# Delta rule: queries convolved after the projection instead of inside it, on ScalarE and VectorE

## The reference, cut to what matters

```python
y = conv_general_dilated(x, w[:, None, :], window_strides=(1,), padding=[(KS - 1, 0)], feature_group_count=C)
return silu(y)                                   # per channel: w[0]*x[t-3] + w[1]*x[t-2] + w[2]*x[t-1] + w[3]*x[t]
...
q = conv_silu(x @ Wq, conv_q).reshape(bsz, seq_len, H, KD)      # H = 8 heads, KD = 128
k = conv_silu(x @ Wk, conv_k).reshape(bsz, seq_len, H, KD)
v = conv_silu(x @ Wv, conv_v).reshape(bsz, seq_len, H, VD)      # VD = 32
q = l2norm(q)
k = l2norm(k)
def step(state, inp):                            # scanned over the tokens
    retained = einsum('bhvk,bhk->bhv', state, k_t)
    state = a4 * (state - b4 * rk) + b4 * vk     # rk, vk: outer products of retained and of v_t with k_t
    o_t = einsum('bhvk,bhk->bhv', state, q_t)
```

## Time and profile before

| | us |
|---|---|
| median of 3 runs | 4452.96 (4449.75 to 4459.58) |
| the profiled execution: its own time | 4450.96 |
| its span, first to last instruction | 4449.0 |
| TensorE busy in the span | 3796.8 (85%) |
| VectorE | 2365.0 (53%) |
| ScalarE | 1509.0 (34%) |
| GpSimd | 736.4 (17%) |
| taps (L2008): 1024 records, first and last start | 2768.5 and 4225.0 |
| mean granted TensorE clock over the span | 0.808 |

### The profile page before, as it was taken

One profiled execution on the slowest core, in us unless ns is written; L12 is line 12 of the kernel. 1 busy time (PEld: TensorE's weight loads), 2 busy tenths in 40 slices (PEclk: granted clock), 3 DMA queues, 4 the chain that ended last, 5 costly groups with the idle time before them and its releaser, 6 DMA issues. The chain is left out here.

```text
span 4449.0 us, 124857 instructions
## 1 busy us (share of the span) xinstructions
PE 3796.8 (85%) x55640; PEld 2398.6 (54%) x55640; DVE 2365.0 (53%) x6027; ACT 1509.0 (34%) x2783; POOL 736.4 (17%) x724
## 2 busy tenths in 40 slices
PE   4877775999948887878787795999999999999986
PEld 2336662444325555556565442566666666666672
DVE  3757773332268777777777111244444444444445
ACT  2643332555432222222222142333333333333323
POOL 1212221000011112121211000222222222222210
PEclk9886666999955556555655697999999999999967
DMA  2000001322000000000000001000000000000000
GB/s 80 0 1 1 1 1 30 47 38 38 17 1 3 3 3 3 3 3 3 3 3 3 16 1 58 1 2 2 2 2 2 2 2 2 2 2 2 2 2 21
DMA packets 18968, 45.93 MB, mean 10 GB/s; under 512 B 4864, under 2 KB 8321, under 8 KB 17409
## 3 DMA queue, kind: packets, MB, share of 16 engines
q1 hardware_dynamic: 18432, 37.95, 3.6%
HBM read 35.71 MB, written 2.23 MB: 9 GB/s over the span
## 5 line engine op out<-in xcount | busy, mean ns | idle before, releaser
L2008 PE MATMUL ps<-d_hp,d_w_qk 128*128 128x512 f32 x1024 | 546.3, 629 | 2.7 <-DVE d_hp L2265 2.7
L1227 PE MATMUL ps<-g_Q,g_K 32*32 32x32 f32 (+1 forms) x12288 | 272.7, 249 | 21.9 <-issue 7.5
L1227 PEld LDWEIGHTS ps<-g_Q,g_K 32*32 32x32 f32 x12288 | 238.3, 136 | 65.0 <-PE ps L1227 39.0
L2086 POOL TENSOR_TENSOR d_sq<-d_QK 128x512 f32<-128x512 f32 x128 | 133.0, 1039 | 763.6 <-ACT d_QK L2128 761.0
L1048 PE MATMUL ps<-ex_hs,w_c_fc 128*128 128x512 f32 x512 | 232.6, 598 | 19.4 <-DVE ex_hs L1014 19.4
L1022 DVE TENSOR_TENSOR ex_r<-ex_r 128x512 f32<-128x512 f32 x128 | 88.4, 692 | 277.1 <-ACT ex_r L1036 277.1
L1036 ACT ACTIVATE ex_r<-ps 128x512 f32<-128x512 f32 x256 | 151.5, 592 | 235.5 <-PE ps L1048 235.5
L1259 PE MATMUL ps<-g_S,g_V 32*64 32x32 f32 x4096 | 161.5, 288 | 81.8 <-DVE g_H L1435 63.4
L1059 PE MATMUL ps<-ex_r,w_c_proj 128*128 128x512 f32 x512 | 230.0, 592 | 0.0
L2008 PEld LDWEIGHTS ps<-d_hp,d_w_qk 128*128 128x128 f32 x1024 | 162.7, 191 | 82.2 <-issue 63.4
L2106 ACT ACTIVATE d_F<-ps 128x128 f32<-128x128 f32 x256 | 70.9, 277 | 379.5 <-PE ps L1922 378.4
(11 more groups left out here) (467 smaller groups left out, 8040.8 us busy)
## 6 DMA issues: line engine op xcount, KB each, us to landing
ex_root<-gate_rows SPq DMA_DIRECT2D x8, 2048.0 KB, 15.1
d_QK<-in_conv_qk_dram SPq DMA_DIRECT2D x2, 2048.0 KB, 8.2
X<-in_x_dram SPq DMA_DIRECT2D x1, 2048.0 KB, 10.8
w_c_fc<-in_c_fc_dram SPq DMA_DIRECT2D x1, 2048.0 KB, 8.0
w_c_proj<-in_c_proj_dram SPq DMA_DIRECT2D x1, 2048.0 KB, 12.4
out_dram<-X SPq DMA_DIRECT2D x1, 2048.0 KB, 6.3
w_wmod<-in_wmod_dram SPq DMA_DIRECT2D x1, 1536.0 KB, 6.4
w_w<-in_w_dram SPq DMA_DIRECT2D x2, 768.0 KB, 5.0
```

Source lines behind the costliest of these rows:

```text
L1227: ins = e.matmul(later(scored, n_), keys_, queries(n_, planes, r, 4 * i + j), start=(turn_ == 0 and part == 0 and n_ != 1), stop=(part == ...
L2008: ins = e.matmul(b, w_qk[:, j, c, ts(H, C)], hp_of(u)[:, j:j + T], start=(j == 0), stop=(j == TAPS - 1))
L2086: e.tensor_tensor(squares(x), qk, qk, ALU.mult).then_inc(pool.steps, pool.did(f"{tag}sq{x}"))
```

## The change

The queries' weights stay unweighted (`d_w_q`), and a query head is projected by one matmul. The convolution is applied to its result: ScalarE copies the PSUM bank into an SBUF row `d_conv`, scaled by the last tap; VectorE adds the three other taps, each reading the bank shifted by one, two or three columns; Silu then reads `d_conv` in place of the bank. The keys keep their four taps. The query product stands at step 3, a turn earlier than the first query tap stood. The copy stands at step 4 ahead of the inversion's place, the three additions at the ends of steps 4, 5 and 7. The bank of the queries is freed by the last addition, `d_conv` by the Silu. Of the two small stages only the one of the keys is left, and `conv_q`, 16 KB, is loaded with the stage's other weights.

```diff
-        w_qk = k.sb("d_w_qk", [C, TAPS, 2, 8 * C], stack=s)
+        w_q, w_k = k.sb("d_w_q", [C, 8 * C], stack=s), k.sb("d_w_k", [C, TAPS, 8 * C], stack=s)
+        cv = k.sb("d_conv", [C, T], stack=s)[:]
...
-        for n in range(2):
+        for n in (1,):
...
+                    e.tensor_copy(w_q[:], w_plain[:, 0]).then_inc(dve.steps, dve.did())
                     e.wait_ge(dma.steps, dma.at("taps"))
                     for j in range(TAPS):
-                        e.tensor_tensor(w_qk[:, j, n], w_plain[:, n], taps[:, j], ALU.mult).then_inc(dve.steps, dve.did())
+                        e.tensor_tensor(w_k[:, j], w_plain[:, n], taps[:, j], ALU.mult).then_inc(dve.steps, dve.did())
...
                     turn = NI * (x // 8) - 50 + x % 8
-                    put(u, turn, "taps", x, place={8: 0, 0: 0, 1: 1}.get(turn % NI, 2))
+                    if x % 8 == 0:
+                        put(u, turn - 1, "taps", x)
+                    elif x % 8 >= 4:
+                        put(u, turn, "taps", x, place={8: 0, 0: 0, 1: 1}.get(turn % NI, 2))
+                for x in range(0, 8, 2):
+                    for j in range(TAPS):
+                        put(u, NI * (x // 2) - 50 + (0, 0, 1, 3)[j], "conv", TAPS * x + j, place=(1 if j == 0 else 2))
...
+                            if c == 0:
+                                if x == 0:
+                                    e.wait_ge(dve.steps, dve.at(f"u{u - g}nh"))
+                                if u or run:
+                                    e.wait_ge(dve.steps, dve.at(f"{tag}conv{TAPS * run - 5}" if run else f"u{u - 1}conv27"))
+                                e.matmul(b, w_q[:, ts(H, C)], hp_of(u)[:, 3:3 + T], start=True, stop=True).then_inc(pe.steps, pe.did(f"{tag}run{run}"))
+                                return
...
+                        elif what == "conv" and x % TAPS == 0:
+                            run = x // TAPS
+                            e.wait_ge(pe.steps, pe.at(f"{tag}run{run}"))
+                            if u or run:
+                                e.wait_ge(act.steps, act.at(f"{tag}run{run - 2}" if run else f"u{u - 1}run6"))
+                            e.activation(cv, tap_bank(run), ACT.Copy, scale=k.w["conv_q"][:, 4 * g + run // 2, 3:4]).then_inc(act.steps, act.did(f"{tag}conv{x}"))
...
+                            if x % 2 == 0:
+                                e.wait_ge(dve.steps, dve.at(f"{tag}conv{TAPS * x + 3}"))
...
+                        elif what == "conv" and x % TAPS:
+                            run, late = x // TAPS, x % TAPS
+                            if late == 1:
+                                e.wait_ge(act.steps, act.at(f"{tag}conv{TAPS * run}"))
+                            else:
+                                e.wait_ge(dve.steps, dve.at(f"{tag}conv{x - 1}"))
+                            e.scalar_tensor_tensor(cv[:, late:], tap_bank(run)[:, 0:T - late], k.w["conv_q"][:, 4 * g + run // 2, 3 - late:4 - late], cv[:, late:],
+                                                   ALU.mult, ALU.add).then_inc(dve.steps, dve.did(f"{tag}conv{x}"))
```

More of the change, by code:

```diff
@@ L122 @@
     "gla": ["W_in2", "b_in2", "W_qka", "b_qka", "W_v2", "b_v2", "W_y2", "b_y2", "W_out2", "b_out2", "h0", "gla_mask"],
-    "delta": ["Wv3", "Wg3", "Wab3", "Wo3", "A_log", "dt_bias", "conv_v", "o_norm_w", "joins", "eye32", "upto3", "ones3", "picks"],
+    "delta": ["conv_q", "Wv3", "Wg3", "Wab3", "Wo3", "A_log", "dt_bias", "conv_v", "o_norm_w", "joins", "eye32", "upto3", "ones3", "picks"],
     "mix": ["W_r3", "W_k3", "W_v3", "mu"],
@@ L2003, in prepare @@
                             c, H, b = run % 2, 4 * g + run // 2, tap_bank(run)
-                            if x == 0:
-                                e.wait_ge(dve.steps, dve.at(f"u{u - g}nh"))
+                            if c == 0:
[5 more added lines that the diff above has]
+                                return
                             if j == 0 and (u or run > 1):
                                 e.wait_ge(act.steps, act.at(f"{tag}run{run - 2}" if run > 1 else f"u{u - 1}run{run + 6}"))
-                            ins = e.matmul(b, w_qk[:, j, c, ts(H, C)], hp_of(u)[:, j:j + T], start=(j == 0), stop=(j == TAPS - 1))
+                            ins = e.matmul(b, w_k[:, j, ts(H, C)], hp_of(u)[:, j:j + T], start=(j == 0), stop=(j == TAPS - 1))
                             if j == TAPS - 1:
@@ L2125, in prepare @@
                                          ACT.Silu).then_inc(act.steps, act.did(f"{tag}values{x}"))
-                        elif what == "taps_done":
-                            e.wait_ge(pe.steps, pe.at(f"{tag}run{x}"))
-                            e.activation(QK[:, x % 2, 4 * (u % 3) + x // 2], tap_bank(x), ACT.Silu).then_inc(act.steps, act.did(f"{tag}run{x}"))
+                        elif what == "conv" and x % TAPS == 0:
[4 more added lines that the diff above has]
+                            e.activation(cv, tap_bank(run), ACT.Copy, scale=k.w["conv_q"][:, 4 * g + run // 2, 3:4]).then_inc(act.steps, act.did(f"{tag}conv{x}"))
+                        elif what == "taps_done":
+                            if x % 2 == 0:
+                                e.wait_ge(dve.steps, dve.at(f"{tag}conv{TAPS * x + 3}"))
+                            else:
+                                e.wait_ge(pe.steps, pe.at(f"{tag}run{x}"))
+                            e.activation(QK[:, x % 2, 4 * (u % 3) + x // 2], cv if x % 2 == 0 else tap_bank(x), ACT.Silu).then_inc(act.steps, act.did(f"{tag}run{x}"))
                         elif what == "gate" and x == 0:
@@ L2584, in layouts @@
     o["Wqk3"] = c(np.stack([i["L3_attn_Wq"], i["L3_attn_Wk"]], 1))
+    o["conv_q"] = c(i["L3_attn_conv_q"].reshape(8, C, 4).transpose(1, 0, 2))
     o["conv_qk"] = c(np.stack([i["L3_attn_conv_q"].T, i["L3_attn_conv_k"].T], 0))
```

1 line of the change is left out of this document (added).

## The result

| | before | with the change |
|---|---|---|
| median of the runs | 4453.89 (4449.75 to 4459.58, 4 runs) | 4305.27 (4297.02 to 4313.89, 4 runs) |
| the profiled execution: its own time | 4450.96 | 4297.02 |
| its span | 4449.0 | 4295.1 |

The ratio is 0.9664, with a 95% interval of 0.9647 to 0.9681. The forecast was 4367, the range 4285 to 4460. In a second set of five runs the changed kernel took 4306.16 (4295.86 to 4307.85).

What follows compares the result with a forecast made beforehand. TensorE's stream was taken to bound the kernel. From 4451 us, 64 cycles x (24.0 - 22.87) = 72 and the setup's 12 give 84 less: 4367 us, range 4285 to 4460.

Steps and rivals of the forecast that it cites:

- What bounds the kernel: Delta stage: TensorE's stream of work sets the time, busy 1377.74 of 1402 us at a granted clock of 0.99.
- The taps removed: Delta stage: three fewer wide products a cycle, 0.86 us each, take 2.58 us from a cycle, 165 us in all.
- the waits put back: Delta stage: new TensorE waits where taps were cover or additions collide, 0.65 us a cycle together.
- The 0.5 at step 6: End of step 6: without its tap TensorE waits 0.5 us for d_X, charged in every cycle.
- The additions: ScalarE's copy at 0.67 us and VectorE's three multiply-adds at 0.75 us each; neither engine becomes the bound.
- The 0.15 a cycle for collisions: Before d_W: where the norms' exponentials or output scaling share the cycle, the additions don't fit; 0.15 us a cycle charged.
- The setup, 12 us: Before the delta stage: one of two tap stages goes, its DMA and four multiplies, 12.8 us; net 12 us less.
- The clock: Delta stage: 10% of time at 1.2 GHz, between 2% and 30%, so a cycle takes 22.9 us, not 21.9.
- rival 1: Delta stage: the clock stays as it is, waits as forecast; 134 us less, 4317 us; chance 0.2.
- Rival 3: Delta stage: four tapless turns pull the clock down; at 30% a cycle takes 25.1 us, 4509 us; chance 0.15.
- Rival 2: Delta stage: the added operations come late, so d_W and all behind it slip; about 4412 us; chance 0.13.
- rival 4: Taps were not the bound, or new waits equal them; only the setup shows: 4440 to 4450 us; chance 0.05.

Runs made afterwards that it cites:

- The run with the inversion first: VectorE does the inversion's subtraction and transpose ahead of its part of making the next matrix at steps 0 and 6, against the changed kernel: 4541.3 us.

## Why the prediction was right, and where it was off

**What bounds the kernel.** Right. A wide product added costs 1.0 us, 0.86 of which is its stream; elementwise work taken away (no convolution) gives back about 5 us. TensorE's stream sets the time.

**The taps removed, 2.58 us a cycle, and the waits put back, 0.65.** Right as a sum: at full clock a cycle loses 2.01 us (1.97 by the second trace) where 2.58 - 0.65 = 1.93 was forecast, from 23.80 (forecast 23.8) to 21.79 (forecast 21.9). The 0.5 at step 6 is in the trace as placed: 0.51 us, 38 times. But it comes in 38 of 58 cycles: in none but one of those with the gate sums, and in only half of those right after them. The forecast charged it in every cycle, 0.5; it is 0.33 a cycle. All of TensorE's named waits together went from 19.3 us before to 50.0 in 58 cycles each, 0.53 a cycle more: besides the 19.4 at step 6 the wait on d_OT grew from 3.5 to 9.8, and one on d_sq of 4.4 came. The prediction did not name these two, and they stay in the run without the additions.

**The additions.** Right in price (0.748, 0.682) and in that d_W is not late. The 0.15 a cycle for collisions is a little over the 0.1 that leaving them out gave.

**The setup, 12 us.** Right: 12.8 us between the two rounds of multiplies, and 12.1 by the medians of the run that put the stage back. The 15.2 of the main trace is 2.4 more by the chance of one DMA.

**The clock: the step that was off.** The prediction took 10% of the stage at 1.2 GHz, from ends of 2% (as now) and 30% (a straight line by the number of taps). Measured is 1.2% in one trace of the changed kernel and 3.0% in the other. With the first in the prediction's own formula a cycle takes 1 / (0.988/21.9 + 0.012/38) = 22.0, and the sum is 64 x (24.0 - 22.0) + 12 = 140, 4311 us; with the second it is 22.2 and about 4324. So this one term makes most of the 62 us, 43 to 56. What was wrong is the line between the two stretches: it took the share to grow tap by tap from five taps to none. With four wide products a cycle in the right places it still is 1.9%, and with four in the wrong places 35%. So their number alone does not set it. The branch that the forecast rested on, 4320 to 4400 us with a tenth of the stage at the lower clock, did not happen; what happened was rival 1, which had a chance of 0.2, and the range was wide enough to hold it.

**Rival 3** is real, and was given the wrong trigger. The price is of the size forecast (25.1 us a cycle and 4509 us at 30%): three runs have cycles of 25 to 26 us at shares of 29 to 47%, and times of 4500 to 4541. But four turns without a query tap did not set it off. What the runs in which the clock fell have in common is a wait of TensorE in 31 cycles or more, that is 1.1 us or longer at its longest, ahead of a stretch of small products: on d_ze (three runs) or on the first d_X (two). In the runs where it stayed, the waits that come as often are 0.7 us at most, and those of 1.4 us come in 15 cycles at the most. This is what they share, not a cause shown. The run with the inversion first shows that no matmul has to go: another order on VectorE is enough. Whether the wait acts by itself or by what stands around it stays open; so does why one key product at step 8 costs 132 us less than one at step 2. No run here took the wait on d_ze away while the tap of step 8 was missing, which would have told it.

The Trainium skill (TensorE: Matmul & The Clock Gate, section Why this matters for your kernels) asks that TensorE not be left idle for long between bursts. For this change it gave the better forecast: 4317 against 4367. That section would not have warned of the rest: with the key tap of step 8 gone the longest wait is 1.4 us and TensorE is busy 95% of the time, and the clock still fell to 0.83. So the measurements agree with the rule for the change, and they show that keeping it is not enough.

**Rivals 1, 2 and 4.** Rival 1 is what happened, with the waits of the forecast. Rival 2 falls with the missing wait on d_W and with the run without the convolution, rival 4 with the doubled product.

## What to carry to other kernels

A wide matmul in an in-order queue is work and cover at once: before taking it out, find what is prepared behind it, and take out the one behind which the least is pending (here step 2's, worth 39 us, where step 8's cost 195). Where such a product can be moved, put it into the longest wait that comes in most cycles. And judge TensorE's clock by running the pattern, since neither the count of wide products nor the busy share told which variant would lose it.

## What the runs showed of the hardware that was not expected

- The granted clock fell to 0.83 to 0.86 over the stage with TensorE busy 94 to 95% of it, and to 0.76 with one key product at step 2 (busy 91%). Two kernels with the same matmuls (the change and its variant with the inversion first) had 1.2 to 3.0% and 29% of the time at 1.2 GHz.
- Once the pattern loses the clock it does so again and again: the kernel with one key product at step 2 has 42 separate stretches at 1.2 GHz between 2830 and 4060 us, 580 us in sum, the longest 17 us; the changed kernel has two of 6.8 us in one trace, and eight, 34 us in sum, in the other.
- A multiply-add of 128 x 512 fp32 with one tensor in PSUM and a pointer scalar takes 0.75 us in a stage where GpSimd is busy a quarter of the time (330.89 of 1266 us), and with 509 columns 0.747, as good as the same. With both tensors in SBUF, in another stage, it had been 1.757; what makes that difference was not tested.
